# Self-attention with a compressive memory: heads and query groups exchanged on the probability tile, outputs on 32x32 tiles of the array, and a ones column in the values

## The reference

```python
B, S, _ = x.shape            # 64, 32, 128
q = x @ Wq ; k = x @ Wk ; v = x @ Wv                 # k and v have 8 heads of 8, q has 16
q4 = q.reshape(B, S, 16, 8)
k4 = jnp.repeat(k.reshape(B, S, 8, 8), 2, axis=2)
v4 = jnp.repeat(v.reshape(B, S, 8, 8), 2, axis=2)
scores = jnp.einsum('bsnd,btnd->bnst', q4, k4) * 8 ** -0.5
probs = jax.nn.softmax(scores, axis=-1)
a_dot = jnp.einsum('bnst,btnd->bsnd', probs, v4)
sigma_q = jax.nn.elu(q.reshape(B, S, 2, 64))
a_mem = ((sigma_q @ memory) / (sigma_q @ memory_norm)[..., None]).reshape(B, S, 16, 8)
w = jax.nn.sigmoid(memory_weight)
x = x + (a_dot * (1.0 - w) + a_mem * w).reshape(B, S, 128)
```

## Time and profile before

| | us |
|---|---|
| three timed runs | 1193.25, 1198.02, 1201.19; median 1198.02 |
| the profiled execution | 1191.41, of it 1188.8 span (first to last instruction) |
| the stage's loop in the profiled execution | 283.98 (first GpSimd instruction) to 389.74 (end of the last L904): 105.8 |

### The profile page before, as it was taken

The page is one execution under the profiler, slowest core; times in us unless marked ns, Lnnn a source line. Parts: engine busy times, 40 slices in busy tenths (PEclk is TensorE's granted clock), DMA queues, the critical chain, the costliest instruction groups (busy, mean ns, idle before and its releaser), DMA issues. The chain is left out here.

```text
span 1188.8 us, 38609 instructions
## 1 busy us (share of the span) xinstructions
PE 1028.6 (87%) x14222; PEld 806.9 (68%) x14222; DVE 779.0 (66%) x2840; ACT 711.5 (60%) x1725; POOL 402.8 (34%) x756
## 2 busy tenths in 40 slices
PE   5899999986767758887799999999999999887965
PEld 2688888853766547876578888888888887422443
DVE  3578888865687378884475666666656666365376
ACT  2588888853676437774465555555555554464467
POOL 0122222206452036664143434343434344112042
PEclk8799999998899679998899999999999999998978
DMA  1443334300000826664354545454545453000001
GB/s 52 117 122 80 80 80 80 80 11 1 1 1 2 310 78 197 216 195 128 86 127 114 132 118 131 121 128 118 130 113 135 114 130 105 28 0 0 1 1 35
DMA packets 71676, 109.83 MB, mean 92 GB/s; under 512 B 12512, under 2 KB 51360, under 8 KB 71424
## 3 DMA queue, kind: packets, MB, share of 16 engines
q1 hardware_dynamic: 69056, 103.06, 32.1%
q0 software_dynamic: 2496, 5.12, 1.6%
HBM read 92.79 MB, written 15.34 MB: 91 GB/s over the span
## 5 line engine op out<-in xcount | busy, mean ns | idle before, releaser
L1533 POOL TENSOR_TENSOR d_p<-d_p,d_rtotal 128x289 f32<-128x289 f32 x256 | 170.2, 665 | 254.8 <-DVE d_rtotal L1677 254.8
L1637 ACT ACTIVATE d_p<-d_p,d_nmax 128x289 f32<-128x289 f32 x256 | 137.7, 538 | 131.6 <-DVE d_nmax L1671 131.5
L1671 DVE CUSTOM_DVE_ANT_0 d_p<-bank,d_low 128x289 f32<-128x289 f32 x256 | 112.1, 438 | 150.6 <-PE bank L1564 150.6
L1578 PE MATMUL bank<-d_pT,d_xr 32*128 32x128 f32 x5120 | 160.9, 275 | 2.1 <-DVE d_a L1691 2.1
L1564 PE MATMUL bank<-x_keyT,d_q 128*128 128x289 f32 x512 | 158.2, 426 | 2.9 <-DVE d_nmax L1671 1.6
L1578 PEld LDWEIGHTS bank<-d_pT,d_xr 32*128 32x128 f32 x5120 | 148.8, 187 | 11.0 <-issue 3.9
L438 ACT ACTIVATE a_p<-a_p,a_nmax 128x257 f32<-128x257 f32 x256 | 116.2, 506 | 33.5 <-DVE a_nmax L475 31.7
L1685 DVE STREAM_TRANSPOSE d_pT<-d_p 128x320 f32<-128x320 f32 x256 | 128.1, 500 | 1.1 <-POOL d_p L1533 1.1
L475 DVE CUSTOM_DVE_ANT_0 a_p<-bank,a_low 128x257 f32<-128x257 f32 x256 | 93.8, 422 | 25.7 <-PE bank L388 23.7
L1564 PEld LDWEIGHTS bank<-x_keyT,d_q 128*128 128x128 f32 x512 | 82.0, 189 | 37.0 <-DVE d_nmax L1671 21.7
L445 ACT ACTIVATE a_pT<-bank 128x512 f32<-128x512 f32 x128 | 69.7, 594 | 20.6 <-PE bank L397 20.1
(11 more groups left out here) (334 smaller groups left out, 2105.4 us busy)
## 6 DMA issues: line engine op xcount, KB each, us to landing
d_xr<-key_rows SPq DMA_DIRECT2D x256, 160.0 KB, 3.1
d_low<-mask_low SPq DMA_DIRECT2D x64, 144.5 KB, 3.4
a_ctT<-in_ctxT SPq DMA_DIRECT2D x64, 128.5 KB, 2.1
a_low<-mask_low SPq DMA_DIRECT2D x64, 128.5 KB, 3.0
c_ct<-in_ctx SPq DMA_DIRECT2D x32, 256.0 KB
key_rows<-c_ct SPq DMA_DIRECT2D x32, 256.0 KB, 2.2
c_w<-in_L_ffn_w SPq DMA_DIRECT2D x8, 578.0 KB, 10.4
c_w<-expert_out SPq DMA_DIRECT2D x8, 256.0 KB, 4.5
```

What stands on the lines that cost most here:

```text
L1533: nc.gpsimd.tensor_tensor(p, p, rtotal[:, b % 2, g:g + 1].broadcast_to([128, KEYS]), ALU.mult).then_inc(normed, 1)
L1578: ins = nc.tensor.matmul((OL if latents else O)[j], xr[rows, b % 2, k, :], pT[rows, b % 2, :, 32 * k:32 * k + 32], start=(k == 0 or latent ...
L1637: nc.scalar.activation(p, p, ACT.Exp, bias=nmax[:, b % 2, g:g + 1], scale=-1.0, accum_out=total[:, b % 2, g:g + 1]).then_inc(exp_made, 1)
L1671: nc.vector.tensor_tensor_reduce(P[:, b % 2, g, 0:KEYS], S[u % 2], low[:, b % 4, :], -1.0, 3.4e38, ALU.add, ALU.min, accum_out=nmax[:, b % ...
```

## The change

Heads and groups are exchanged: a partition of the score tile is now a (group, query) pair and the row holds (batch, head, key). The keys are masked by head and the queries by group (and scaled). After the transpose, partition 32h+k, column 32g+q holds head h, group g. The outputs of a head and a group are then a product of 32 keys by 32 queries with 8 value columns: one 32x32 tile of the array. A ninth column of ones in `v` gives the sum of the probabilities, so nothing is normalised before the outputs; VectorE divides afterwards and turns the 32x32 blocks itself.

What goes: L864, L866, L868 (sum, inverse, multiply of 512 elements), L785 (four masks), L873 (head sum), and four of the 128x128 products. What comes, in each step: 64 products of 32x32 with 9 columns, a reciprocal of 16 elements in PSUM, a 128-element multiply from PSUM, a 128-element transpose. The scores have one PSUM bank in place of two, the outputs four banks (one for each head) in place of one, numerator and spread share one bank. Outputs follow one step behind, not two. The memset of `v` is 288 elements a row in place of 1024. The memory's spread is due 4 steps after its chunk's start, not 5, the weighing 5, not 6.

```diff
-            vb = sb("b_vb", [128, 2, 4, 128])
+            v = sb("b_v", [128, 2, 4, 4, DH + 1])
-            S = [core.bank[:, n, :].rearrange("p (c k) -> p c k", k=LAT) for n in (0, 1)]
-            TP, OP, VP = (core.bank[:, n, :].rearrange("p (b k) -> p b k", b=4) for n in (2, 3, 4))
+            S = core.bank[:, 0, :].rearrange("p (c k) -> p c k", k=LAT)
+            TP, VP = (core.bank[:, n, :].rearrange("p (b k) -> p b k", b=4) for n in (1, 2))
+            OP = core.bank[:, 4:8, 0:4 * (DH + 1)].rearrange("p h (b d) -> p b h d", b=4)
-            NUM, SPREAD = core.bank[:, 5, :], core.bank[:, 7, :]
+            NUM, SPREAD = core.bank[:, 3, :], core.bank[:, 3, :]
...
             @block.tensor
...
-                def scores(i, j, first):
-                        pe.wait_ge(shifted, n - 1)
+                def scores(n):
+                        pe.wait_ge(shifted, n)
...
+                def output(n):
                     pe.wait_ge(t_copied, n + 1)
                     pe.wait_ge(v_copied, n + 1)
+                    if n >= 1:
+                        pe.wait_ge(o_scaled, n)
...
                     for b in range(4):
-                        ins = nc.tensor.matmul(OP[:, b, :], vb[:, j % 2, b, :], pT[:, j % 2, b, :], start=True, stop=True)
+                        for g in range(4):
+                            for h in range(4):
+                                rows, cols = slice(32 * h, 32 * h + 32), slice(32 * g, 32 * g + 32)
+                                ins = nc.tensor.matmul(OP[cols, b, h, :], pT[rows, n % 2, b, cols], v[rows, n % 2, b, g, :], start=True, stop=True)
...
                         if c:
-                            pe.wait_ge(num_kept, c)
+                            pe.wait_ge(weighed, c)
...
+                for n in range(GROUPS):
+                    if n >= 1:
+                        transposes(n - 1)
+                    scores(n)
+                    if n >= 1:
+                        output(n - 1)
+                    values(n)
+                    retrieve(n)
+                transposes(GROUPS - 1)
+                output(GROUPS - 1)
...
             @block.scalar
...
-                def masked(i, j, first=False):
...
+                for n in range(GROUPS + 1):
+                    if n >= 1:
+                        values(n - 1)
+                        transposed(n - 1)
+                    if n < GROUPS:
+                        retrieve(n)
+                        tokens(n)
+                        exponential(n)
+                        features(n)
...
             @block.vector
...
-                def normalise(i, j):
...
-                    nc.vector.tensor_reduce(aT[:, bass.ds(n * 128, 128)].rearrange("p (b q) -> p b q", b=4),
-                                            odiag[:, j % 2].rearrange("p b h q -> p b q h"), AXX, ALU.add).then_inc(o_copied, 1)
+                def output(n):
+                    dve.wait_ge(o_made, n + 1)
+                    nc.vector.reciprocal(rtotal[:].rearrange("p (b h) -> p b h", b=4), OP[:, :, :, DH]).then_inc(o_inverted, 1)
...
+                    nc.vector.tensor_tensor(orow[:].rearrange("p (b h) d -> p b h d", b=4), OP[:, :, :, 0:DH],
+                                            rtotal[:].rearrange("p (b h) -> p b h", b=4).unsqueeze(3).broadcast_to([128, 4, 4, DH]), ALU.mult).then_inc(o_scaled, 1)
+                    dve.wait_ge(o_scaled, n + 1)
+                    nc.vector.transpose(aT[:, 128 * n:128 * n + 128], orow[:].rearrange("p c d -> p (c d)")).then_inc(o_turned, 1)
+                for n in range(GROUPS):
+                    invert(n)
+                    shift(n)
+                    if n >= 1:
+                        output(n - 1)
+                    retrieve(n)
```

More of the change, by code:

```diff
@@ L746, in retrieve @@
                         ins.then_inc(spread, 1)
-                def body(i, first, last):
-                    for j in range(2):
-                        if not first:
-                            transposes(i, j - 2)
-                        scores(i, j, first)
-                        if not first:
-                            output(i, j - 2)
-                        values(i, j, first)
-                body(0, True, False)
-                transposes(1, -2, True)
-                scores(1, 0, False)
```

203 lines of the change are left out of this document (71 added, 132 removed).

## The result

The changed kernel takes 1205.26 us (median of 18 runs, 1198.80 to 1210.43), the kernel before 1199.23 (18 runs, 1193.25 to 1204.61) on the same chip. The ratio is 1.0044, 95% interval 1.0027 to 1.0061: slower by 0.3 to 0.6%, within the 1% that the prediction called no change, but outside its range and on the other side of its forecast of 10 us less. In the profiled execution (span 1206.6 us) the loop lasts from 283.91 to 399.75, 115.8 us against 105.8. The rest of the difference between the two profiled spans lies outside the loop, in stages that the change doesn't touch, and isn't explained here; an experiment's second profile of the changed kernel has a loop of 112.5 us.

A forecast was written before the change was run, and what follows sets the result against it. It took chains between engines, with none full, to bound the loop. Start, steps and tail summed to -10.35 us; instruction supply +1 and faster products -1 left -10.4, from 1198.0 to 1187.6 us, range 1180 to 1203.

The forecast's parts named there:

- Prices: Expected instruction costs in the loop: outputs block 1.34 us, VectorE's three new instructions together 0.82 us, value copies 0.264 each.
- Rival 2: Small outputs products cost more than forecast, 29 ns a pair or 3.7 us a block: about +20 us, 1218; chance 0.09.
- Start: Start of the loop: a smaller memset, about 0.3 us instead of 0.95, with ScalarE and GpSimd behind it: -0.65 us.
- Steps 0 to 3: First steps, 16.7 us before, partly at half clock: no gain taken, +0.3 us for outputs moved into the cold time.
- The cycle of three steps at full clock: Spread step 4.7, numerator step 6.2 and feature step 5.2 us: 16.1 against 17.9, 1.8 us less.
- steps 12 to 15: Late loop steps where no chunk begins and one spread is left: 13.1 us against 15.5, -2.4 us.
- the tail: Serial work after step 15: 7.1 us, or 8.3 with 1.2 more at half clock, against 13.0: -4.7 us.
- rival 4: More gain than forecast: full clock in steps 3 to 9, no instruction stops, first cycle gains: -16 us, 1182; chance 0.12.
- The same disturbance 1.7 twice: Steps 3 to 9: two cycles, 32.2 us, plus the old kernel's half-clock disturbance, gave 35.6 against 36.7, -1.1 us.
- Rival 3: TensorE's clock falls more often in the loop; slower than before from about 25 us at half, likeliest 1215; chance 0.06.
- Supply of instructions: Unrolled outputs, 1,920 more instruction pairs each run once, stop TensorE for instructions: +1 us.
- rival 1: Ends gain, cycle does not: one instruction stop per outputs block (8 us) or dearer value copies: -4 us, 1194; chance 0.25.

The follow-up runs named there:

- e2: The changed kernel with each step's outputs as four 128x128 products on a constant matrix, so not the attention's outputs: 1172.48 us against 1191.05 for the kernel before.
- e8: The changed kernel with outputs as 16 products of 128x32 weights and 36 columns, values block-diagonal by head, everything computed: 1181.59 us against 1192.32 for the kernel before.
- e3: The changed kernel with every small outputs product done twice: 1262.27 us, ratio to the kernel before 1.0568 to 1.0655.
- e5: The changed kernel with 16 outputs products of 32x32 and 36 columns, batches 1 to 3 using batch 0's probabilities: 1184.89 us against 1200.22 for the kernel before.
- e1: The changed kernel run again unedited, as a reference: 1196.27 us against 1191.05 for the kernel before.
- e6: The changed kernel with outputs as four 128x128 products of 36 columns on a constant matrix, not the real outputs: 1190.53 us, ratio to before 0.9879 to 0.9954.
- e11: e8 with four full 128x128 products on a constant matrix, never read, in each of two TensorE gaps: 1181.51 us against 1204.86 for the kernel before.
- e12: e8 with seven full, never read products in each of the same two TensorE gaps: 1180.67 us against 1204.86 for the kernel before.
- e7: The changed kernel with outputs as four full products of 144 columns and VectorE's multiply split in four: 1202.29 us, ratio to before 1.0006 to 1.0070.

## Why the prediction was wrong, point by point

- *Prices*: near. The outputs block took 1.16 to 1.18 us at full clock, not 1.34; VectorE's three took 855 ns, not 820. Rival 2 is out. The Trainium skill, TensorEngine Tiling (Array Packing), Performance Considerations, Instruction Overhead, gave 3.2 us a block as an estimate; the measured 1.16 us for 128 pairs does not agree.
- *Start* (-0.65): 283.91 to 289.27 is 5.4 us, before 6.0: right. *Steps 0 to 3* (+0.3): 16.7, as before: right.
- *The cycle of three steps at full clock* (16.1), *steps 12 to 15* (13.1) *and the tail* (8.3): e2 has this cycle without the clock's fall. Its maximum starts at 300.39, 316.53 and 332.76 in steps 3, 6 and 9: 16.1 and 16.2. Steps 12 to 15 take 12.9, the tail is 6.8. That they agree is partly luck, since e2's block is 0.89 us and the working had 1.34. With 0.89 it gives 4.3 + 5.75 + 5.2 = 15.2 for the cycle; e2's outputs blocks lie 4.4, 6.4 and 5.3 apart. The numerator step is the one too short: VectorE does the maximum and the subtraction ahead of the outputs (310.15 to 311.48 in e2) and begins the weighing only at 312.32, 2.4 us behind the block's start; the working had left these two out of that step. In the same way rival 4's -16 meets e2's 105.8 - 89.7 = 16.1 by a block that is shorter than its own; with the changed kernel's block it would be some 12.6 (16.1 - 3.5).
- *The same disturbance 1.7 twice* is the step that failed. It carried the cold time of the kernel before over to the new one in steps 3 to 9, and steps 9 to 15 got none at all. Steps 3 to 9 took 42.7 us, not 35.6; steps 9 to 12 23.2, not 16.1; 12 to 15 20.8, not 13.1: some 7 us more each, with 58 us of the loop at half clock, where the kernel before had 21. The tail came to 7.1 at full clock and gave 5.9. Sum: -0.6 + 0 + 6.0 + 5.3 + 5.2 - 5.9 = +10.0.
- *Rival 3, the clock stays low*, is what happened, and it had 0.06. Its own price line (slower than before from about 25 us at half, each at up to 0.5) was near: it was 58 us, at 0.35, and the time lies 10 us under the 1215 that it called likeliest. Its chance rested on L410's stage, where 64 loads of 32 columns stood among big products and the clock held:

```profile
40.00:262.00 222.00, 215.70 (x5487) 174.75 (x5485) 173.67 (x825) 176.39 (x380) 46.20 (x190) 0.98 0.33 78
```

But there TensorE was busy 97% of the time (215.7 of 222 us), in this loop 70% before and 83% after. e8, with just L410's weights in this loop, has 37 us at half: a stage with more work around the small products was no evidence for this one.
- *Supply of instructions* (+1): too small. The three stops are 4.5 us, in e3 38. So rival 1's mechanism was there too, at about half of its 8 us. Without the long stops much of the half-clock time stays (e5: 41 us in its loop).
- *GpSimd as the bound* didn't come up: its instructions waited for TensorE as well.
- The marks named ahead of time fit: granted clock 0.5 in more than three stretches, "issue" inside blocks. Of "right" there came VectorE's three instructions and a tail of 7.1 us (about 8 was said); the block, at 1.16, is under its 1.3, the maximum isn't every 16 us, and the numerator's wait for VectorE shows once (0.94).

On the clock: the Trainium skill, TensorE: Matmul & The Clock Gate, section HAM oscillation, tells of clocks that fall since TensorE waits 3 to 5 us for DMA between bursts. Apart from the one ahead of the first scores (5.65 us), no wait of the changed kernel's loop is longer than 2.7 us, so the page's case isn't this one. Here idle time alone doesn't order the kernels (17 to 21 us in e1, e2, e5, e6, e8 and the changed one, with 7 to 58 us at half). That less waiting raises the clock, as the filled gaps of e11 and e12 show, agrees with the page, but is only a part.

## What to carry over

Before cutting a full product into small ones because most of what comes out is thrown away, count what the full one does for TensorE's clock: here the swap itself was nearly even (1.18 us a block for 0.89), and what it did to the clock cost some 18 us by the working above, of which nothing shows in the price of the small products. Read the granted clock of the loop as a term of the sum with its own price (here 0.25 to 0.46 us for each at half), and don't carry the old kernel's cold time over when the kind of its products changes. Where TensorE waits anyway and the clock falls, full products on constants in the gap are a cheap test, and here a gain.

## What was not expected of the hardware

- The clock fell with TensorE less idle (32 to 20 us, 21 to 58 at half). With block length, instructions and waits the same, 36 columns in place of 128 took the time at half clock in the loop from 7 to 19 us (e6 and e2), and by 21 ± 11 us over all timed runs.
- A pair of instructions on a 32x32 tile takes 9.1 ns at full clock, and hardly more at half (1.30 us a block against 1.16), while full products double (0.97 to 1.83).
- Long runs of instructions that each run once stop: for 1.0 to 2.7 us seventeen times, 38 us with the short ones, in a loop with 256 pairs a step (e3), where 36 loads of 16 KB came over the instruction queue. The Trainium skill, Runtime: NRT & Kernel Launch, Instruction fetch mechanics, calls the fetching mostly hidden; at 9 ns a pair it isn't here, while with 8 pairs a block (e2) no such stop shows in it.
- VectorE takes 287 ns on 32 partitions for what takes 291 on 128 (e7 and the changed kernel).
